# One order of score, row and sum matmuls for all four cross attentions of a gated Flamingo stack

## The reference

```
for l in range(4):
    x = x + tanh(g_xattn[l]) * cross_attention_l(layernorm(x), ctx)
    x = x + tanh(g_ffn[l])   * ffn_l(layernorm(x))
```

```
q, k, v = heads(x @ Wq), heads(ctx @ Wk), heads(ctx @ Wv)
out = softmax(q @ k.T / sqrt(8)) @ v          # per batch and head
return heads_joined(out) @ Wo
```

## Time and profile before

| what | value |
|---|---|
| median of three runs | 3145.81 us |
| profiled execution | 3153.18 us |
| its span, first to last instruction | 3151.4 us |
| PE matmul busy | 2724.9 us (86%) |
| DVE busy | 2025.1 us (64%) |
| ACT busy | 1985.0 us (63%) |
| POOL busy | 1581.5 us (50%) |
| mean granted TensorE clock | 0.945 |
| cross attention of layers 0, 1, 2, 3 | about 175, 208, 166, 164 us |

### The profile page before, as it was taken

One profiled execution on the slowest core, in us unless ns is written; L12 is line 12 of the kernel. 1 busy time (PEld: TensorE's weight loads), 2 busy tenths in 40 slices (PEclk: granted clock), 3 DMA queues, 4 the chain that ended last, 5 costly groups with the idle time before them and its releaser, 6 DMA issues. The chain is left out here.

```text
span 3151.4 us, 74744 instructions
## 1 busy us (share of the span) xinstructions
PE 2724.9 (86%) x27218; PEld 1724.5 (55%) x27218; DVE 2025.1 (64%) x3872; ACT 1985.0 (63%) x5960; POOL 1581.5 (50%) x1845
## 2 busy tenths in 40 slices
PE   4896999799988998899889998899879977996895
PEld 1553766366745775477647664677524433652552
DVE  3664887488847885688658874787445534755673
ACT  3344888488857887588858884888523333555343
POOL 0423887188827884588638881788223102410430
PEclk9798999999999999999999999999979988998797
DMA  2001000100010001000010001000100000000000
GB/s 96 1 2 44 17 19 17 41 17 17 19 39 18 17 17 38 20 17 18 14 44 17 17 19 40 17 17 17 34 7 2 1 1 0 2 2 0 1 2 14
DMA packets 35860, 58.58 MB, mean 19 GB/s; under 512 B 7184, under 2 KB 32656, under 8 KB 33808
## 3 DMA queue, kind: packets, MB, share of 16 engines
q1 hardware_dynamic: 35472, 53.52, 5.4%
HBM read 27.28 MB, written 1.05 MB: 9 GB/s over the span
## 5 line engine op out<-in xcount | busy, mean ns | idle before, releaser
L1037 POOL TENSOR_TENSOR l_qk<-l_ta,l_tb 128x256 f32<-128x256 f32 x768 | 539.5, 739 | 114.9 <-DVE l_tb L1091 114.9
L1053 POOL TENSOR_TENSOR l_qk<-l_qk,l_rn 128x512 f32<-128x512 f32 x384 | 392.8, 1044 | 217.0 <-DVE l_rn L1113 217.0
L660 POOL TENSOR_SCALAR qmr<-q_all,cf 128x256 fp32r<-128x256 f32 x128 | 116.2, 925 | 718.7 <-SPq L461 380.0
L692 DVE TENSOR_REDUCE mrow<-ring 128x2 f32<-128x512 f32 x512 | 324.5, 685 | 190.8 <-PE ring L508 182.1
L958 ACT ACTIVATE l_pr<-st,l_mn 128x128 f32<-128x128 f32 x1152 | 407.6, 383 | 38.6 <-DVE l_mn L1079 38.6
L1044 POOL TENSOR_TENSOR l_pr<-l_pr,l_rs 128x512 f32<-128x512 f32 x384 | 393.8, 1052 | 42.5 <-DVE l_rs L1103 42.5
L645 ACT ACTIVATE pt<-st 128x512 f32<-128x512 f32 x384 | 200.2, 600 | 286.6 <-PE st L543 286.6
L1095 DVE TENSOR_REDUCE l_n<-l_sq 128x8 f32<-128x512 f32 x384 | 262.9, 686 | 177.4 <-ACT l_sq L967 175.1
L958 ACT ACTIVATION_READ_ACCUMULATOR l_pr<-st,l_mn 128x1 f32 x1152 | 255.4, 222 | 0.0
L821 PE MATMUL ring<-l_wa,l_xs 128*128 128x512 f32 x384 | 201.2, 648 | 42.3 <-DVE l_xs L1074 28.5
L533 PE MATMUL st<-qm,k_all 32*128 32x512 f32 x1024 | 219.8, 664 | 0.0
(11 more groups left out here) (237 smaller groups left out, 6370.3 us busy)
## 6 DMA issues: line engine op xcount, KB each, us to landing
l_vm<-l_v SPq DMA_DIRECT2D x192, 96.0 KB, 2.0
l_wa<-in_wa SPq DMA_DIRECT2D x7, 2048.0 KB, 9.2
l_vm<-l_v SPq DMA_DIRECT2D x192, 32.0 KB, 1.9
l_wf<-in_wf SPq DMA_DIRECT2D x6, 580.5 KB, 4.5
w<-in_w SPq DMA_DIRECT2D x1, 2752.0 KB, 15.8
cf<-in_cf SPq DMA_DIRECT2D x1, 1253.0 KB, 7.7
x<-in_xT SPq DMA_DIRECT2D x1, 1024.0 KB, 5.2
ctxT<-in_ctxT SPq DMA_DIRECT2D x1, 1024.0 KB, 9.7
```

The costliest lines, as they stand in the source:

```text
L692: dve.tensor_reduce(mrow[b % 2][:, t, j, 2 * p:2 * p + 2], bank_of(f"R{r}").rearrange("p (h k) -> p h k", h=2), AX.X, ALU.max).then_inc(ri ...
L1037: ins = pool.tensor_tensor(halves[0][:, :, x], halves[1][:, :, x], halves[2][:, :, 1 - x], ALU.add)
L1053: pool.tensor_tensor(part, part, t.rn[:, :, 4 * x:4 * x + 4].unsqueeze(3).broadcast_to([P, 2, 4, LHD]), ALU.mult).then_inc(qk_normed, 1)
```

## The change

`MASKED_PERIOD` becomes the only `PERIOD`, used by all four layers, and `run_of_scores` issues every run step by step: all opens, all adds, all subtractions. The prologue keeps its form. A full period now has four runs of four S items, the first two with three R items and the last two with two; R3, R7, R10 R11 and R14 R15 stand between pairs of quarters; Q4 to Q7 are done in the batch's own period, behind T, and not at the start of the next. The ring's order changes with it: R12 and R13 come before T.

```diff
-PERIOD = ("q4 q5 q6 q7 R0 R1 S0 R2 S1 S2 S3 q8 R3 R4 q9 q10 q11 S4 S5 R5 R6 R7 S6 S7 q12 q13 q14 q15 V S8 R8 R9 "
-          "S9 S10 S11 R10 Q0 Q1 R11 R12 Q2 Q3 O T S12 R13 S13 S14 S15 R14 R15").split()
-MASKED_PERIOD = ("S0 S1 S2 S3 R0 R1 R2 q8 q9 R3 q10 q11 S4 S5 S6 S7 R4 R5 R6 q12 q13 R7 q14 q15 V "
-                 "S8 S9 S10 S11 R8 R9 Q0 Q1 R10 R11 O Q2 Q3 S12 S13 S14 S15 R12 R13 T Q4 Q5 R14 R15 Q6 Q7").split()
+PERIOD = ("S0 S1 S2 S3 R0 R1 R2 q8 q9 R3 q10 q11 S4 S5 S6 S7 R4 R5 R6 q12 q13 R7 q14 q15 V "
+          "S8 S9 S10 S11 R8 R9 Q0 Q1 R10 R11 O Q2 Q3 S12 S13 S14 S15 R12 R13 T Q4 Q5 R14 R15 Q6 Q7").split()
...
-RING_PLANS = [ring_plan(MASKED_PERIOD if l == 1 else PERIOD) for l in range(4)]
+RING_PLAN = ring_plan(PERIOD)
...
-                for part in ([items] if l == 1 else [[i] for i in items]):
-                    for kind, n in part:
-                        if kind == "S":
-                            open_scores(b, n)
-                        else:
-                            open_rows(n)
-                    for kind, n in part:
-                        if kind == "S":
-                            add_scores(b, n)
-                        else:
-                            add_rows(n)
-                    for kind, n in part:
-                        if kind == "S":
-                            subtract_maxima(b, n)
+                for kind, n in items:
+                    if kind == "S":
+                        open_scores(b, n)
+                    else:
+                        open_rows(n)
+                for kind, n in items:
+                    if kind == "S":
+                        add_scores(b, n)
+                    else:
+                        add_rows(n)
+                for kind, n in items:
+                    if kind == "S":
+                        subtract_maxima(b, n)
```

More of the change, by code:

```diff
@@ L444, in cross_attention @@
     first = l * NB
[L445 to L448, removed]
+    order, order_at, order_dve = RING_PLAN
+    ring0, ring0_dve = l * len(order), l * order_dve[-1]
     has_bias = l in (1, 3)
@@ L603, in _ @@
             for b in range(NB):
-                for run in runs_of(period):
+                for run in runs_of(PERIOD):
                     kind, n = run[0][0], int(run[0][1:] or 0)
@@ L617, in _ @@
                         project_back(b - 1)
-            for n in (int(item[1:]) for item in period if item[0] == "q"):
+            for n in (int(item[1:]) for item in PERIOD if item[0] == "q"):
                 sum_values(NB - 1, n)
@@ L735, in _ @@
             for b in range(NB):
-                for item in period:
+                for item in PERIOD:
                     if item[0] == "R" and row_item(b, item) < 16 * NB:
```

## The result

The changed kernel takes 3160.38 us in the median of 20 runs (lowest 3153.32), the kernel before 3149.41 in 20 runs beside it. The ratio is 1.004, 95% interval [1.0026, 1.0053]. One of the 20 runs of the changed kernel (3295.55 us, at a mean granted clock of 0.804) stood in a slower state and is left out of the ratio. The forecast was 3149.3 us, a ratio of 1.001, and no measurable difference.

What follows compares the result with a forecast made beforehand. The prediction took PE to set the pace. Changes of +0.3 us each in layers 0 and 3, +2.9 in layer 2 and 0 in layer 1, together +3.5 on the median 3145.81, gave 3149.3 us; range 3137 to 3162, 8 in 10.

Steps and rivals of the forecast that it cites:

- PE's cost of the new order: Steady period of layer 0: PE alone would need 17.53 us a batch, 0.83 under the old 18.36.
- The two waits of the steady period: Layer 0: stalls of 0.32 us ahead of Q0 and 0.48 ahead of the next S0 run, making the period 18.33.
- Layer 2: Steady period of layer 2, with pad matmuls: 19.15 us against 18.96, +0.2 a period, +1.0 over five.
- The end: Layers 0 and 3: last but one period 17.2 us, -0.55; last batch +0.2 from waiting for four banks at once.
- The first batch: Start of layers 0, 2 and 3: uncovered waits make it longer by 0.8 us in layers 0 and 3, 2.0 in layer 2.
- a rival with 0.16: First batch of layers 0, 2 and 3: idle PE gets its full clock later, +12 us, so 3161; chance 0.16.
- the first rival: Steady periods: the waits don't bite and PE's 17.53 shows, about -9.5 us, so 3136; chance 0.16.
- the third: Rival on ring waits: every run opening R items starts 0.2 us later, up to +6 us, so 3155; chance 0.12.
- The sum: All cross attentions: +0.3 us each in layers 0 and 3, +2.9 in layer 2, together +3.5.

Runs made afterwards that it cites:

- e3: The changed kernel, but in layers 0, 2 and 3 a run opens and adds its S items before opening R items; ratio 0.9995 to the kernel before.
- c1_again: The changed kernel, unaltered, profiled a second time; layer 3's first-batch window took 25.04 us against 23.61 in the kernel before.
- h1: The changed kernel with a block of 36 filler matmuls before batch 0 of layers 0, 2 and 3; only batch 0 read, full clock lost for 6.8 to 10.2 us.
- h5: The kernel before, issued step by step, with 36 filler matmuls before batch 0 of layers 0, 2 and 3; only batch 0 read, clock lost for 3.4 to 6.8 us.
- e2: The kernel before with its old list, but all layers issue each run step by step; ratio 1.0029 to the kernel before.
- e4: The changed kernel, but batch 0 of layers 0, 2 and 3 is issued item by item; ratio 1.001 to the kernel before.
- e5: The changed kernel with filler matmuls before and between items of the prologue and batch 0 in layers 0, 2 and 3; ratio 1.011 to the kernel before.

## Why the prediction was wrong, step by step

- **PE's cost of the new order**: right. The run is 1.54 without masks too, and a period without the ring wait is 17.85 (e3), which is 17.53 and the 0.32 ahead of Q0.
- **The two waits of the steady period**: right in place and size, 0.53 for 0.48 and 0.32 for 0.32. The period came out at 18.45, in the bounds of 18.33 to 18.5; the bank's delay was at the far one of its two values, 0.82 for 0.75.
- **Layer 2**: right in sign, +0.39 a period for +0.2.
- **The end**: 16.9 for 17.2 in the last but one period of layers 0 and 3, and +0.8, -0.1 and +0.3 in the last batch for +0.2 each.
- **The first batch**: the step that failed, +11.9 us for +3.6. I walked its waits at a clock taken from the kernel before ("clock up during it, as before") and put its change into a rival with 0.16. The clock was up 3.6, 9.0 and 3.1 us later, where that rival wanted 4 in each layer, and this makes about 7 of the 11.9 us. The waits make the remaining 5 and were under-sized too (1.4 for 0.8 in c1_again's layer 3). In layer 0 the walk itself held up to the S8 run within 0.5 us. The rival named the stands in their right size (three of 0.5 to 1.2 us; in layer 0 four of 0.3 to 1.3). Its argument against itself, that V comes at nearly the same time, was no argument: V came 0.7 us later in layer 0 and the clock 3.6. I also sized layer 2's share by waits alone (+2.0); it was +5.8, with the clock 9 us later.
- **The rivals' sums** hold two slips. The terms written out for the first rival (-0.8 x 10, -0.45 x 5, +2) add up to -8.3 and not -9.5, so 3137.6 us for 3136. In the third, four times 0.2 a period would be 0.8 and not the 0.4 that its +6 uses. Neither enters the forecast.
- **The sum** would have been 3.5 + 8.3 = 11.8 with this term right; the medians differ by 11.0. The forecast time of 3149.3 rested on the median of three runs, 3145.81; that of 20 is 3149.41, so part of the distance to 3160.38 is the base.

## What to carry to other kernels

When work is reordered at a place where TensorE's clock is still low, walk the start of each stage apart from its steady state, and take the clock there as an outcome and not as given: here the order with more short stands on PE also had its clock later. Gather waits only over items whose banks come free together; an S item that is ready should not stand behind the bank of an R item that comes after it, and putting the ready group first took the whole steady wait away. A steady period that is nearly unchanged, as here, says nothing of the eighth of the work at either end.

## What the runs showed of the hardware

- In the kernel before, layer 0, the granted clock stayed at 1.2 GHz for the 15.2 us from 100.22 to 115.40, though PE counted as busy for 14.87 of them; apart from V all its matmuls there were on 32-row groups. Two executions of one kernel gave the full clock at the same place within 0.1 us in five cases of six; in the sixth it came 3.4 us earlier.
- The full clock fell after PE had stood for 0.54 us and then during a stand of 1.38 us (h1, layer 0), once after stands of 0.2, 0.5 and 0.2 us only (h5, layer 2), and lived through one of 1.52 us elsewhere (e2, layer 0).
- One us of low clock cost 0.45 us in the first batch (0.38 between two layers of e4), near the 0.5 that it would if PE alone set the pace.
- Full-array filler of 256 columns put singly between 32-row matmuls made an R item and its maximum take 1.05 us for 0.60 (e5). In the changed kernel's steady period a break between 32-row, 32-column and full-array work cost the 0.14 us that the prediction had counted. By the Trainium skill (TensorEngine Tiling (Array Packing), Key Properties) a change of tiling mode drains the engine; the page gives no time for it, and neither number here is of the drain alone.
